# The third mixer channel of pairs 5 to 7 with plain weights, its taps on ScalarE and its sums on GpSimd

## The chip, the cores and the metric

One core of a Trainium2 chip runs the whole program. The metric is the device time of one execution in microseconds (us); before the change it is 496.37 us as the median of 3 runs (495.74 to 497.36). All work is in fp32 or in pairs of rounded fp32 parts.

## The reference, cut to what matters

One decoder layer over 16 sequences of 128 tokens with 128 features. The first block is the mixer: a projection to three channels of 128 features, a causal convolution of 3 taps over each channel, a product, a causal convolution of 4 taps, a gate and an output projection. Its sum with x is normalised and goes to a self attention and a cross attention (16 heads of 64 each), a feed-forward part and a last block of experts.

```python
x = einsum('bld,de->ble', u, W_in) + b_in
uc = dw_causal_conv(swapaxes(x, 1, 2), short_w, short_b)   # 3 taps, zeros before the start
q, k, v = uc[:, :D], uc[:, D:2*D], uc[:, 2*D:]
v = dw_causal_conv(k * v, inner_w, inner_b)                # 4 taps
y = einsum('bld,de->ble', swapaxes(q * v, 1, 2), W_out) + b_out
```

## The kernel before, in words

The mixer works on pairs of sequences (m = 0 to 7, 256 columns). The attentions work on items, one for each sequence of each attention: p = 0 to 31, 0 to 15 are self attention. Each engine has its own program, written out by hand in order, and a loop over turns p. The order of the calls is the order of execution on that engine; semaphores tie the engines together. The first five mixer pairs are started early, and the rest of the mixer is spread over the turns 0 to 10.

In turn p TensorE (PE in the profile) makes queries, keys and values of later items (`unit`, `v_half`), the transposes of item p-1's probabilities (`transposes`, line 570), the scores of item p+1 (`scores`, line 587), and P times V of item p-1 (`p_v`, line 602). VectorE (DVE) takes the score maxima of item p+1 (`maxima`, line 1172), ScalarE (ACT) its exponentials (`exps`, line 871, four heads a call), DVE the reciprocals of the sums (line 1182), and GpSimd (POOL) multiplies the probabilities by them (`normalise`, line 1574, four calls of 128x512 an item). `transposes` of item p in turn p+1 begin only when all maxima of item p+2 are made (line 568), since both use banks 2 and 3.

Of the mixer: channels 0 and 1 of pair m are projected in turn 2m-8, channel 2 in turn 2m-7 (`projection`). So pairs 5, 6 and 7 have their channels 0 and 1 in turns 2, 4, 6 and channel 2 in turns 3, 5, 7. Channels 0 and 2 use bank 4, channel 1 bank 5; `p_v` writes both banks, so it waits for the evictions (line 597). There are two ways to the 3 taps:

- With weights that hold the taps (w3): nine matmuls of 256 columns, three shifted inputs times three products of high and low parts (lines 652 to 654), one eviction by ACT with a bias (line 944), and a repair of the first two columns on POOL (`edges`, line 1620).
- With plain weights: three matmuls (lines 72 to 74), three evictions by ACT with the tap as scale (`projected`, lines 939 and 941), and two sums on POOL (`add_taps`, line 1644). `TAPPED` = 5: pairs 5 to 7 do so, but only their channels 0 and 1.

On POOL `keys_values(m)` stands at the end of turn 2m-7, behind the four `normalise` of that turn: sums of channel 1, repair of channel 2, the product KV (line 1636), sums of channel 0. Behind it come `output_bias`, `affine` and `next_residual` of the next turn, and that turn's `normalise`. On DVE `inner_convolution(m)` (lines 1269 and 1273, four instructions of 128x256) stands in turn 2m-6, behind the last `pt_out`, and ahead of that turn's last reciprocals and of the next item's maxima. `x_low` (line 1246) stands on DVE in odd turns ahead of `residual` and the last reciprocals; it needs `x_high` (line 926), which stands on ACT behind the eviction of channel 2 and `exps(p, 3)`.

## Time and profile before

| | |
|---|---|
| median of 3 runs | 496.37 us (495.74 to 497.36) |
| profiled execution, whole time | 495.88 us |
| its span, first to last instruction | 493.8 us |
| PE busy | 469.6 us (95%) |
| DVE busy | 380.1 us (77%) |
| ACT busy | 374.0 us (76%) |
| POOL busy | 271.1 us (55%) |
| granted TensorE clock, mean | 0.987 |
| shares of the chain that ended last | PE 68%, DVE 14%, ACT 9%, issue 5%, POOL 1% |

Busy time counts each engine by itself. The chain follows the end of the program back through whatever released each step, so a share in it is time that the end waited on. A timeline row gives start, duration, engine, line, operation and operands; in brackets stands how long the engine was idle before it and who ended that. The start of an instruction can lie a little before the end of the one ahead on the same engine.

### The profile page before, as it was taken

How to read it: one execution, taken by the hardware profiler on the slowest of the kernel's cores; microseconds unless marked ns; L12 is line 12 of the kernel's file. 1: busy time of each engine (PE TensorE's matmuls, PEld its weight loads, DVE VectorE, ACT ScalarE, POOL GpSimd, SP SyncE). 2: the span in 40 equal slices, each digit the busy share in tenths (PEclk: the TensorE clock that was granted, in tenths of full speed). 3: DMA queues.
4: the chain of work that ended last, by engine and by line, in shares of the span. 5: the costliest groups of instructions: out<-in, count | busy, mean ns of one | idle time of the engine just before them, and what ended most of it. 6: DMA issues, size and time to landing. Idle time of an engine off the chain costs nothing.

```text
span 493.8 us, 14159 instructions
## 1 busy us (share of the span) xinstructions
PE 469.6 (95%) x4632; PEld 431.1 (87%) x4632; DVE 380.1 (77%) x1828; ACT 374.0 (76%) x1407; POOL 271.1 (55%) x396
## 2 busy tenths in 40 slices
PE   7778999999999999999999999999999999999993
PEld 7778888989899999999999999999999998798872
DVE  3678778888888877887787777777777777647884
ACT  4547898888877788877778887777777776754866
POOL 5556357876768554555545455444444455534553
PEclk9899999999999999999999999999999999999996
DMA  8750000000000004000000000000000000600003
GB/s 233 239 206 1 1 3 1 2 2 2 1 3 2 2 2 126 2 3 1 3 1 2 2 2 3 1 2 2 2 2 2 1 4 1 171 24 0 9 12 101
DMA packets 15688, 14.58 MB, mean 30 GB/s; under 512 B 2816, under 2 KB 13056, under 8 KB 15488
## 3 DMA queue, kind: packets, MB, share of 16 engines
q1 hardware_dynamic: 14008, 13.19, 8.9%
q8 instruction: 38, 0.62, 0.6%
q10 hardware_dynamic: 1608, 0.49, 0.4%
q14 instruction: 34, 0.28, 0.2%
HBM read 12.23 MB, written 1.44 MB: 28 GB/s over the span
## 4 chain that ended last, share of the span: by engine, by line
PE 68%; DVE 14%; ACT 9%; issue 5%; POOL 1%; DMA 1%; ACTq 0%; SPq 0%; DVEq 0%; POOLq 0%
PE late_bank L570 9%; PE late_bank L618 9%; PE late_bank L587 9%; PE late_bank L602 8%; PE late_bank L72 8%; PE late_bank L73 7%; PE late_bank L74 7%; ACT P L871 5%; DVE P L1172 4%; PE late_bank L305 3%; DVE G L1273 1%; PE late_bank L627 1%; DVE at_PT L1198 1%; PE late_bank L652 1%; DVE at_k L1190 1%
## 5 line engine op out<-in xcount | busy, mean ns | idle before, releaser
L871 ACT ACTIVATE P<-P,at_negmax 128x128 f32<-128x128 f32 x512 | 199.0, 397 | 75.0 <-DVE at_negmax L1172 75.0
L1574 POOL TENSOR_TENSOR P<-P,at_inv 128x512 f32<-128x512 f32 x128 | 136.7, 1079 | 114.4 <-DVE at_inv L1182 114.3
L1198 DVE COPY at_PT<-late_bank 128x512 f32<-128x512 f32 x128 | 87.7, 688 | 35.6 <-PE late_bank L570 35.4
L1172 DVE CUSTOM_DVE_ANT_0 P<-late_bank,maskb 128x128 f32<-128x128 f32 x512 | 110.4, 286 | 2.5 <-PE late_bank L587 2.5
L871 ACT ACTIVATION_READ_ACCUMULATOR P<-P,at_negmax 128x1 f32 x512 | 100.3, 196 | 0.0
L570 PE MATMUL late_bank<-ident,P 128*128 128x128 f32 x512 | 76.3, 273 | 2.5 <-DVE at_negmax L1172 1.8
L570 PEld LDWEIGHTS late_bank<-ident,P 128*128 128x128 f32 x512 | 59.7, 140 | 9.1 <-issue 4.5
L587 PE MATMUL late_bank<-at_k,at_q 64*128 64x128 f32 x1024 | 65.8, 279 | 0.9 <-DVE at_k L1190 0.9
L602 PE MATMUL late_bank<-at_PT,V 128*64 128x128 f32 x1024 | 63.0, 276 | 2.0 <-ACT C L941 2.0
L587 PEld LDWEIGHTS late_bank<-at_k,at_q 64*128 64x128 f32 x1024 | 59.7, 188 | 4.8 <-issue 1.2
L602 PEld LDWEIGHTS late_bank<-at_PT,V 128*64 128x64 f32 x1024 | 55.3, 137 | 5.9 <-issue 2.4
L1190 DVE COPY at_k<-late_bank 128x512 f32<-128x512 f32 x64 | 44.1, 690 | 5.7 <-PE late_bank L74 4.8
L1172 DVE DVE_READ_ACCUMULATOR2_ANT at_negmax<- 128x1 f32 x512 | 42.7, 83 | 0.0
L1592 POOL TENSOR_TENSOR at_N<-at_N,row_ln_g 128x128 f32<-128x128 f32 x32 | 14.7, 460 | 48.4 <-DVE at_N L1223 48.4
L881 ACT ACTIVATE at_q<-late_bank 128x512 f32<-128x512 f32 x64 | 37.5, 586 | 2.3 <-PE late_bank L74 2.3
L890 ACT ACTIVATE V<-late_bank 128x512 f32<-128x512 f32 x64 | 37.5, 585 | 0.0
L898 ACT ACTIVATE at_OT<-late_bank 128x512 f32<-128x512 f32 x64 | 34.2, 586 | 2.9 <-PE late_bank L602 2.9
L618 PE MATMUL late_bank<-wo_sa,at_OT 128*128 128x128 f32 x256 | 31.4, 276 | 0.6 <-DVE x1T_lo L1309 0.6
L618 PE MATMUL late_bank<-wo_ca,at_OT 128*128 128x128 f32 x256 | 31.2, 275 | 0.0
L618 PEld LDWEIGHTS late_bank<-wo_sa,at_OT 128*128 128x128 f32 x256 | 29.9, 192 | 1.2 <-issue 1.2
L618 PEld LDWEIGHTS late_bank<-wo_ca,at_OT 128*128 128x128 f32 x256 | 29.9, 192 | 0.1
L1182 DVE RECIPROCAL at_inv<-at_total 128x4 f32<-128x4 f32 x128 | 21.6, 171 | 10.1 <-ACT P L871 9.9
(213 smaller groups left out, 1068.6 us busy)
## 6 DMA issues: line engine op xcount, KB each, us to landing
ctxT_raw<-in_ctxT SPq DMA_DIRECT2D x1, 1024.0 KB, 8.6
out<-xres SPq DMA_DIRECT2D x4, 224.0 KB, 2.5
x<-in_xT SPq DMA_DIRECT2D x1, 768.0 KB, 11.1
xres<-in_x SPq DMA_DIRECT2D x1, 768.0 KB, 14.7
tap_rows<-in_short_wT SPq DMA_DIRECT2D x3, 192.0 KB, 4.6
sa_wq_raw<-in_sa_wq SPq DMA_DIRECT2D x1, 512.0 KB, 7.9
sa_wk_raw<-in_sa_wk SPq DMA_DIRECT2D x1, 512.0 KB, 9.7
sa_wv_raw<-in_sa_wv SPq DMA_DIRECT2D x1, 512.0 KB, 11.7
```

Of the source, the lines that this page charges most:

```text
L72: nc.tensor.matmul(out, w.hi[wsel], x.hi[xsel], start=first, stop=False)
L570: last = nc.tensor.transpose(banks[T_BANK[g % 2]][:, h * 128:(h + 1) * 128], P[:, n % 2, HQ * g + h, :], k.ident[:])
L587: last = nc.tensor.matmul(score_bank(h), q[rows, t % 2, h // 2, pair], kk[rows, t % 2, h // 2, pair], start=True, stop=True)
L602: last = nc.tensor.matmul(banks[O_BANK[h // 8]][part:part + 64, h // 2 % 4 * 128:(h // 2 % 4 + 1) * 128], V[:, n % 2, h * DH:(h + 1) * DH] ...
L618: last = nc.tensor.matmul(banks[W_BANK][:, 0:128], OT[:, n % 2, c, :], out_w[att(n)][:, c, :], start=(c == 0), stop=(c == H // 2 - 1))
L871: last = nc.scalar.activation(P[:, n % 2, h, :], P[:, n % 2, h, :], ACT.Exp, scale=-1.0, bias=negmax[:, n % 2, h:h + 1], accum_out=total[: ...
L881: nc.scalar.activation(q[:, t % 2, u:u + 2, :], banks[UNIT_BANK[0]][:].rearrange("p (h l) -> p h l", h=2), ACT.Copy, scale=NEG_SCALE).then ...
L890: nc.scalar.activation(V[:, n % 2, half * 512:(half + 1) * 512], banks[V_BANK][:], ACT.Copy).then_inc(v_ok, 1)
L1172: last = nc.vector.tensor_tensor_reduce(P[:, n % 2, h, :], score_bank(h), k.maskb[:, cols(n)], scale=1.0, scalar=3.0e38, op0=ALU.add, op1= ...
L1190: nc.vector.tensor_copy(kk[:, t % 2, u - 1:u + 1, :], banks[UNIT_BANK[1]][:].rearrange("p (h l) -> p h l", h=2)).then_inc(k_ok, 1)
L1198: nc.vector.tensor_copy(PT[:, HQ * g:HQ * g + HQ, :], banks[T_BANK[g % 2]][:].rearrange("p (h l) -> p h l", h=HQ)).then_inc(pt_ok, 1)
L1574: nc.gpsimd.tensor_tensor(tile, tile, inv[:, n % 2, HQ * g:HQ * g + HQ].unsqueeze(2).to_broadcast([128, HQ, 128]), ALU.mult).then_inc(norm ...
```

## The change

Channel 2 of pairs 5 to 7 takes the plain way too: three matmuls instead of nine, three evictions on ACT instead of one, and two sums on POOL instead of the repair. `keys_values` now makes the sums of channel 1, then of channel 2, then KV. The tap tiles lose their two spare columns, so the shifted part is written at an offset and the rest stays zero; there are six of them instead of four, all cleared by POOL at the start, and the plain weights are split for 384 columns instead of 256. In the turns 2, 4 and 6 `exps(p, 3)` moves on ACT from between the evictions of channel 0 and channel 1 to behind both.

```diff
--- before.py
+++ after.py
@@ -162,6 +162,7 @@
 def allocate_projected(k, early):
 
     k.projected_tiles = k.sb(early, "C", [128, 2, 3, PAIR, L]), k.sb(early, "G", [128, PAIR, L])
+    k.late_tap = k.sb(early, "tapped21", [128, PAIR, L])
 
 
 def allocate_context_high(k, ctx):
@@ -231,8 +232,8 @@
     bias = k.sb(mixer, "conv_bias", [128, 3])
     edge = k.sb(mixer, "edge", [128, 3, 2])
     tap_b = k.sb(mixer, "tap_b", [128, 3, 3])
-    k.plain_w = k.split(mixer, "plain_w", [128, 2 * D])
-    k.tapped = tuple(tuple(k.sb(mixer, f"tapped{c}{j}", [128, PAIR, L + 2]) for j in range(2)) for c in range(2))
+    k.plain_w = k.split(mixer, "plain_w", [128, 3 * D])
+    k.tapped = [k.sb(mixer, f"tapped{i}", [128, PAIR, L]) for i in range(5)]
     inner = k.sb(mixer, "inner", [128, 4])
     inner_b = k.sb(mixer, "inner_b", [128, 1])
     KV = k.sb(mixer, "KV", [128, PAIR, L + 3])
@@ -366,7 +367,7 @@
             ctx, "ff", "gained_ok x4_ok z_normal_ok z_half_ok out_ok last_ok last_half_ok blank")
         moved, ze_last, shift_e_ok, minus_e_ok = k.sems(ctx, "ff", "moved ze_last shift_e_ok minus_e_ok")
         plain_hi, plain_lo, tapped_ok, blank_taps = k.sems(ctx, "mx", "plain_hi plain_lo tapped_ok blank_taps")
-        plain_w, tapped = k.plain_w, k.tapped
+        plain_w, tapped = k.plain_w, (k.tapped[0:2], k.tapped[2:4], (k.tapped[4], k.late_tap))
         block = ctx.enter_context(nc.Block())
 
         LN3, OUTER, INNER_NORM, OUT = 0, 1, 2, 3
@@ -641,7 +642,7 @@
                     wait(pe, c_ok, (3 * m, 3 * m, 3 * m + 1)[c])
                 if c == 1:
                     wait(pe, r1_ok, m - 1)
-                if c < 2 and m >= TAPPED:
+                if m >= TAPPED:
                     pe.wait_ge(plain_lo, 1)
                     now = np.s_[:, m % 2, :, 2:2 + L]
                     mm_split(nc, two(c_bank(m, c)), plain_w, np.s_[:, c * D:(c + 1) * D], xT, now).then_inc(c_mm, 1)
@@ -932,11 +933,11 @@
                 wait(act, y_ok, m - 1)
                 if m == 0 and c == FIRST_ORDER[0]:
                     act.wait_ge(bias_ok, 1)
-                if c < 2 and m >= TAPPED:
-                    act.wait_ge(blank_taps, 4)
-                    wait(act, tapped_ok, 4 * (m - TAPPED) - 2 * c)
+                if m >= TAPPED:
+                    act.wait_ge(blank_taps, 6)
+                    wait(act, tapped_ok, 6 * (m - TAPPED) - (0, 4, 2)[c])
                     for j in range(2):
-                        nc.scalar.activation(tapped[c][j][:, :, 2 - j:2 - j + L], two(c_bank(m, c)), ACT.Identity,
+                        nc.scalar.activation(tapped[c][j][:, :, 2 - j:], two(c_bank(m, c))[:, :, 0:L - 2 + j], ACT.Identity,
                                              bias=tap_b[:, c, j:j + 1], scale=taps[:, c, j:j + 1])
                     nc.scalar.activation(C[:, m % 2, c], two(c_bank(m, c)), ACT.Identity, bias=short_b[:, c:c + 1],
                                          scale=taps[:, c, 2:3]).then_inc(c_ok, 1)
@@ -1096,11 +1097,9 @@
                 if p == 0:
                     exps(p, 3)
                 projected(pair_of(p, PROJECT), 0)
-                if p % 2 == 0 and p:
-                    exps(p, 3)
                 projected(pair_of(p, PROJECT), 1)
                 projected(pair_of(p, PROJECT - 1), 2)
-                if p % 2:
+                if p:
                     exps(p, 3)
                 if p % 2 and p < NPAIR:
                     x_high((p + PROJECT + 1) // 2)
@@ -1629,9 +1628,9 @@
                     edges(m, np.s_[1:3])
                 else:
                     add_taps(m, 1)
-                    edges(m, np.s_[2:3])
-                    pool.wait_ge(tapped_ok, 4 * (m - TAPPED) + 2)
-                pool.wait_ge(fix_ok, m + 1 + min(m, TAPPED))
+                    add_taps(m, 2)
+                    pool.wait_ge(tapped_ok, 6 * (m - TAPPED) + 4)
+                pool.wait_ge(fix_ok, min(2 * m + 1, 2 * TAPPED))
                 wait(pool, g_ok, m)
                 nc.gpsimd.tensor_tensor(KV[:, :, 3:], C[:, m % 2, 1], C[:, m % 2, 2], ALU.mult).then_inc(kv_ok, 1)
                 if m >= TAPPED:
@@ -1640,16 +1639,16 @@
             def add_taps(m, c):
 
                 for j in range(2):
-                    wait(pool, tapped_ok, 4 * (m - TAPPED) + 2 * (1 - c) + j)
-                    nc.gpsimd.tensor_tensor(C[:, m % 2, c], C[:, m % 2, c], tapped[c][j][:, :, 0:L],
+                    wait(pool, tapped_ok, 6 * (m - TAPPED) + (4, 0, 2)[c] + j)
+                    nc.gpsimd.tensor_tensor(C[:, m % 2, c], C[:, m % 2, c], tapped[c][j][:],
                                             ALU.add).then_inc(tapped_ok, 1)
 
             def plain_weights():
 
                 pool.wait_ge(ld_win, 16)
-                nc.gpsimd.tensor_copy(plain_w.hi[:], w_in[:, 0:2 * D]).then_inc(plain_hi, 1)
+                nc.gpsimd.tensor_copy(plain_w.hi[:], w_in[:]).then_inc(plain_hi, 1)
                 pool.wait_ge(plain_hi, 1)
-                nc.gpsimd.tensor_tensor(plain_w.lo[:], w_in[:, 0:2 * D], f32(plain_w.hi[:]),
+                nc.gpsimd.tensor_tensor(plain_w.lo[:], w_in[:], f32(plain_w.hi[:]),
                                         ALU.subtract).then_inc(plain_lo, 1)
 
             def gate(m):
@@ -1660,7 +1659,7 @@
                     edges(m, np.s_[0:1])
                     pool.wait_ge(fix_ok, 2 * (m + 1))
                 else:
-                    pool.wait_ge(tapped_ok, 4 * (m - TAPPED + 1))
+                    pool.wait_ge(tapped_ok, 6 * (m - TAPPED + 1))
                 pool.wait_ge(g_ok, m + 1)
                 wait(pool, o1_mm, m)
                 nc.gpsimd.tensor_tensor(yT[:], C[:, m % 2, 0], G[:], ALU.mult).then_inc(y_ok, 1)
```

On ScalarE, turns 2 and 3, before (tapped00 to tapped11 are tap tiles of channels 0 and 1, late_bank4 and late_bank5 the mixer's banks, at_q and at_OT tiles of the attention; P is the probabilities):

```order
L939 ACTIVATE tapped01<-late_bank4,tap_b,taps 128x2x128
L941 ACTIVATE C<-late_bank4,short_b,taps 128x256
L871 ACTIVATE P,at_total<-P,at_negmax 128x128 x4
L939 ACTIVATE tapped10<-late_bank5,tap_b,taps 128x2x128
L939 ACTIVATE tapped11<-late_bank5,tap_b,taps 128x2x128
L941 ACTIVATE C<-late_bank5,short_b,taps 128x256
L871 ACTIVATE P,at_total<-P,at_negmax 128x128 x8
...
L944 ACTIVATE C<-late_bank4,conv_bias 128x256
L871 ACTIVATE P,at_total<-P,at_negmax 128x128 x4
L926 ACTIVATE xT_hi<-x1 128x2x128
```

The same stretch of ScalarE in the changed kernel, whose line numbers are one higher here (tapped4 and tapped21 belong to channel 2):

```order
L940 ACTIVATE tapped1<-late_bank4,tap_b,taps 128x2x127
L942 ACTIVATE C<-late_bank4,short_b,taps 128x256
L940 ACTIVATE tapped2<-late_bank5,tap_b,taps 128x2x126
L940 ACTIVATE tapped3<-late_bank5,tap_b,taps 128x2x127
L942 ACTIVATE C<-late_bank5,short_b,taps 128x256
L872 ACTIVATE P,at_total<-P,at_negmax 128x128 x12
...
L940 ACTIVATE tapped4<-late_bank4,tap_b,taps 128x2x126
L940 ACTIVATE tapped21<-late_bank4,tap_b,taps 128x2x127
L942 ACTIVATE C<-late_bank4,short_b,taps 128x256
L872 ACTIVATE P,at_total<-P,at_negmax 128x128 x4
L927 ACTIVATE xT_hi<-x1 128x2x128
```

The last four exponentials of turn 2 now stand with the eight of turn 3 behind the evictions, and two more evictions stand ahead of turn 3's last exponentials and of `x_high`.

On GpSimd, the end of turn 3 and the start of turn 4, before (C is the projected channels, P the probabilities):

```order
L1581 TENSOR_TENSOR at_rstd<-at_mv,half_neg 128x1
L1644 TENSOR_TENSOR C<-C,tapped10 128x256
L1644 TENSOR_TENSOR C<-C,tapped11 128x256
L1620 TENSOR_TENSOR C<-C,edge 128x2x2
L1636 TENSOR_TENSOR KV<-C 128x2x128
L1644 TENSOR_TENSOR C<-C,tapped00 128x256
L1644 TENSOR_TENSOR C<-C,tapped01 128x256
L1673 TENSOR_TENSOR xres<-xres,b_out 128x256
L1592 TENSOR_TENSOR at_N<-at_N,row_ln1_g 128x128
L1595 TENSOR_TENSOR at_X<-at_N,row_ln1_b 128x128
L1601 TENSOR_TENSOR xres<-at_X,row_ca_bo 128x128
L1574 TENSOR_TENSOR P<-P,at_inv 128x512 x4
```

And in the changed kernel, same place:

```order
L1643 TENSOR_TENSOR C<-C,tapped2 128x256
L1643 TENSOR_TENSOR C<-C,tapped3 128x256
L1643 TENSOR_TENSOR C<-C,tapped4 128x256
L1643 TENSOR_TENSOR C<-C,tapped21 128x256
L1635 TENSOR_TENSOR KV<-C 128x2x128
L1643 TENSOR_TENSOR C<-C,tapped0 128x256
L1643 TENSOR_TENSOR C<-C,tapped1 128x256
L1672 TENSOR_TENSOR xres<-xres,b_out 128x256
L1591 TENSOR_TENSOR at_N<-at_N,row_ln1_g 128x128
L1594 TENSOR_TENSOR at_X<-at_N,row_ln1_b 128x128
L1600 TENSOR_TENSOR xres<-at_X,row_ca_bo 128x128
L1573 TENSOR_TENSOR P<-P,at_inv 128x512 x4
```

Two sums of 128x256 have taken the place of the small repair, and everything behind them on this queue, the next turn's four multiplies of P included, stands behind them.

## Rows read from the trace of the kernel before

**Rows 1.** Waits of PE, 60 to 150 us: who waited for whom, total, times, longest

```profile
PE late_bank L602 <- ACT C L941: 2.0, 3, 0.8
PE late_bank L570 <- DVE at_negmax L1172: 1.0, 4, 0.3
```

**Rows 2.** Timeline of PE: projection of channel 2 in turn 3; first transposes of turns 5 and 9

```profile
83.38 0.29 PE L652 MATMUL late_bank<-xT_hi,w_hi 128*128 128x256 f32 x1
...
84.11 0.28 PE L72 MATMUL late_bank<-x1T_hi,sa_wk_hi 128*128 128x256 f32 x1
...
107.03 0.41 PE L570 MATMUL late_bank<-ident,P 128*128 128x128 f32 x2 [0.25 <-DVE at_negmax L1172]
...
161.00 0.41 PE L570 MATMUL late_bank<-ident,P 128*128 128x128 f32 x2
```

**Rows 3.** Timeline of ACT, turns 2 and 3

```profile
71.15 1.02 ACT L939 ACTIVATE tapped<-late_bank,tap_b,taps 128x256 f32<-128x256 f32 x2
...
72.50 0.42 ACT L871 ACTIVATE P<-P,at_negmax 128x128 f32<-128x128 f32 x1
...
84.41 0.47 ACT L944 ACTIVATE C<-late_bank,conv_bias 128x256 f32<-128x256 f32 x1
84.76 0.41 ACT L871 ACTIVATE P<-P,at_negmax 128x128 f32<-128x128 f32 x1
...
86.30 0.42 ACT L926 ACTIVATE xT_hi<-x 128x256 fp32r<-128x256 f32 x1
```

**Rows 4.** Timeline of DVE: last reciprocals of turn 2, x_low of turn 3

```profile
75.88 0.17 DVE L1182 RECIPROCAL at_inv<-at_total 128x4 f32<-128x4 f32 x1
...
87.64 0.40 DVE L1246 TENSOR_TENSOR xT_lo<-x,xT_hi 128x256 fp32r<-128x256 f32 x1
```

**Rows 5.** Timeline of POOL, end of turn 3 and start of turn 4

```profile
91.33 1.45 POOL L1644 TENSOR_TENSOR C<-C,tapped 128x256 f32<-128x256 f32 x2
92.74 0.21 POOL L1620 TENSOR_TENSOR C<-C,edge 128x4 f32<-128x4 f32 x1
93.08 0.73 POOL L1636 TENSOR_TENSOR KV<-C 128x256 f32<-128x256 f32 x1
...
97.38 2.04 POOL L1574 TENSOR_TENSOR P<-P,at_inv 128x512 f32<-128x512 f32 x2
```

**Rows 6.** Timeline of DVE, convolution of turn 4

```profile
99.34 0.40 DVE L1269 TENSOR_SCALAR G<-KV,inner,inner_b 128x256 f32<-128x256 f32 x1
99.78 1.53 DVE L1273 SCALAR_TENSOR_TENSOR G<-KV,inner,G 128x256 f32<-128x256 f32 x3
```

**Rows 7.** Timeline of DVE, convolution of an earlier pair, 42 us

```profile
41.92 0.48 DVE L1246 TENSOR_TENSOR xT_lo<-x,xT_hi 128x256 fp32r<-128x256 f32 x1
42.33 1.12 DVE L1269 TENSOR_SCALAR G<-KV,inner,inner_b 128x256 f32<-128x256 f32 x1
43.49 1.14 DVE L1273 SCALAR_TENSOR_TENSOR G<-KV,inner,G 128x256 f32<-128x256 f32 x1
```

**Rows 8.** Timeline of POOL at the same time

```profile
42.08 2.27 POOL L1574 TENSOR_TENSOR P<-P,at_inv 128x512 f32<-128x512 f32 x2
```

**Rows 9.** Timeline of POOL, turn 8

```profile
152.37 2.04 POOL L1574 TENSOR_TENSOR P<-P,at_inv 128x512 f32<-128x512 f32 x2
```

**Rows 10.** Timeline of DVE, convolution of turn 8

```profile
154.45 0.40 DVE L1269 TENSOR_SCALAR G<-KV,inner,inner_b 128x256 f32<-128x256 f32 x1
```

**Rows 11.** Timeline of POOL, start of the program

```profile
1.75 1.08 POOL L1762 MEMSET tapped<- 128x260 f32 x4
...
4.26 0.72 POOL L1652 TENSOR_TENSOR plain_w_lo<-w_in,plain_w_hi 128x256 fp32r<-128x256 f32 x1
```

**Rows 12.** Timeline of DVE, its first instruction

```profile
5.64 0.56 DVE L1253 TENSOR_TENSOR w_raw<-w_in,tap_rows 128x384 f32<-128x384 f32 x1 [5.64 <-DMA tap_rows<-in_short_wT]
```

**Rows 13.** Timeline of PE: its longest idle time after the start

```profile
16.14 0.35 PE L669 MATMUL late_bank<-w_out,yT 128*128 128x128 f32 x1 [2.19 <-issue]
```

**Rows 14.** Windows: length, busy time of PE, PEld, DVE, ACT, POOL, granted clock, DMA share, GB/s

```profile
17.26:20.68 3.42, 3.06 (x15) 2.77 (x14) 2.63 (x11) 2.19 (x4) 1.45 (x3) 0.50 0.49 136
```

## The prediction

> **What bounds the kernel now.** The page's busy times come first: TensorE is busy 95% of the span, so most turns are bound by it, but the change lies in the turns 2 to 8, and these have to be read by themselves. The waits of TensorE from 60 to 150 us [rows 1] show that it stands still there in two ways: three times before P times V, for the eviction of channel 1 (2.0 us in all), and four times before the first transposes of a turn, for VectorE's maxima (1.0 us in all). The second kind is the telling one. A turn after an even one starts when VectorE is done, as at 107.03 in turn 5 [rows 2]; whatever TensorE gains before that point is only waited away there. In the even turns 2, 4 and 6 the end is therefore set by VectorE, and behind it by ScalarE. In the odd turns 3, 5 and 7 nothing on TensorE waits after that point, and VectorE in its turn waits for TensorE's last keys and transposes. Turn 9 starts its transposes at 161.00 [rows 2] with no wait shown, but hardly any room either: its maxima come from the VectorE queue of turn 8, which is full.
>
> **TensorE, turns 3, 5, 7.** Nine matmuls become three. The last six took from 83.38 to 84.11 [rows 2], 0.73 us; three turns, 2.2 us at most.
>
> **ScalarE, turns 3, 5, 7.** The eviction of channel 2 took one slot of 84.76 - 84.41 = 0.35 us; the three plain ones take 72.50 - 71.15 = 1.35 us [rows 3]. So `exps(p, 3)` and `x_high` come 1.0 us later. ScalarE's queue is full from turn 3's first exponentials on, so these evictions can't start earlier though the bank is full sooner. `x_high` then starts at 87.30 and ends 0.42 us later, 87.72. VectorE's `x_low` started at 87.64 [rows 4], and without the change of ScalarE it would come 0.73 us earlier, since VectorE follows TensorE here. Now it waits for 87.72 plus a few hundredths: 0.12 us later than before. So TensorE's saving in turns 3 and 5 is lost in this wait. It can be worse: the reciprocals directly ahead of `x_low` do come 0.73 us earlier, so GpSimd starts the multiply that they release at about 87.1, and at 1.02 us for one (half of 2.04, [rows 5]) it still runs until about 88.1, when `x_low` wants to start. Whether a VectorE instruction waits for a running GpSimd one is shown at 42 us [rows 7, 8] and priced below. I take 0.4 us of loss for turn 3 and for turn 5 (bounds 0.1 and 0.5); in turn 7 there is no `x_low`, the last exponentials (1.0 us later) still come ahead of their reciprocals, and I take the full gain of 0.73 us (bound: nothing).
>
> The Trainium skill, page "SBUF — State Buffer", section "Who interferes with whom", says that a VectorE instruction with two SBUF inputs contends with a GpSimd instruction that reads SBUF, and that the loser is blocked for the whole instruction. No row here shows it alone for a plain TENSOR_TENSOR of VectorE that comes second: x_low at 41.92 took 0.48 instead of 0.40 us [rows 7, 4], which points the same way. By the rule turns 3 and 5 lose about 0.4 us each; by the bare wait for `x_high` 0.1 us each.
>
> **The moved exponentials, turns 2, 4, 6.** `exps(2, 3)` started at 72.50 [rows 3] and moves behind 1.35 us of evictions, so its last sum is ready near 75.5. The reciprocals that need it start at 75.88 [rows 4]. About 0.3 us of room is left, so the move costs nothing; if the room were gone, each 0.1 us would go straight to the maxima behind them. Its gain is that channel 1 is evicted 1.5 us earlier and P times V no longer waits. I price that gain at nothing: TensorE just reaches the wait for the maxima 0.6 to 0.8 us sooner, and waits there longer.
>
> **GpSimd, end of the odd turns.** The two sums of channel 1 took 91.33 to 92.74, 1.41 us; each of the second pair has to wait for the sum before it, so I take 1.5 us. The repair, 93.08 - 92.74 = 0.34 us less the wait that any KV has, about 0.2 us, goes [rows 5]. Everything behind is 1.3 us later. GpSimd had no idle time up to the two multiplies at 97.38, which ended at 99.42 [rows 5]. They now run from 98.7 to 100.7 (bounds of the shift: 1.1 and 1.5 us). GpSimd itself has room before its third multiply, so on its own queue this costs nothing. But VectorE's convolution starts at 99.34 [rows 6], that is exactly when these multiplies used to end.
>
> What then happens is shown at 42 us. There two such multiplies ran from 42.08 for 2.27 us [rows 8], and the convolution came in between: its first instruction took 1.12 instead of 0.40 us and the second 1.14 instead of 0.49 to 0.51 [rows 7, 6]. Each was held until the running multiply was over. The cost was 0.72 + 0.65 = 1.37 us. In turn 4 the first instruction comes some 0.6 us after the start of the first multiply instead of 0.25, so it is held about 0.35 to 0.5 us, and the second by the second multiply, 0.65 us. I take 1.1 us for each even turn. Below: 0.7 us, if the shift is small and only the second is held; above: 1.37 us.
>
> This sits on VectorE between `pt_out` and the reciprocals and maxima that release turn 5, where TensorE already waits. So the price is paid in full in turns 4 and 6. In turn 8 the same meeting occurs for pair 7: multiplies at 152.37 for 2.04 us [rows 9], convolution at 154.45 [rows 10], again one right behind the other before. Turn 9 has next to no room [rows 2], so I take 1.1 us there as well.
>
> **Start of the program.** Four clearings took 1.03 us [rows 11], 0.26 each; two more add 0.5. The subtraction of 0.72 us and the cast ahead of it grow from 256 to 384 columns, some 0.4 us together by an estimate from the subtraction. It ended at 4.98 and would end near 5.9. VectorE's first instruction starts at 5.64 [rows 12] and has everything behind it; held by the subtraction it loses 0.2 us (bounds: nothing, 0.35).
>
> **The sum.** 0.2 (start) + 2 x 0.4 (turns 3, 5) + 3 x 1.1 (turns 4, 6, 8) - 0.7 (turn 7) = +3.6 us. With the lower bounds 0 + 0.2 + 2.1 - 0.7 = +1.6; with the upper ones 0.35 + 1.0 + 4.1 = +5.5. On the profiled execution's 495.88 us that is 499.5. The median of the runs is 0.49 us above that execution, so the forecast is 500.0 us, with 498.0 to 501.9 as its own range.
>
> **Rivals.**
>
> *Nothing to measure.* The late multiplies don't hold the convolution, or VectorE has room that I don't see; then the terms left are 0.2 + 0.2 - 0.7, about 496.1 us. For it: all added work lies on engines at 55% and 76% busy, and the even turns' gain is waited away in any case. Against it: rows 7 and 8 show the same two instructions held by the same multiplies.
>
> *Faster.* TensorE is the bound in all these turns: the eighteen matmuls (2.2 us) go, and part of the 2.0 us of waits for the eviction [rows 1] too. All of it would be 4.2 us, 492.2; with the matmuls alone 494.2, which I take. For it: 95% busy. Against it: the waits for the maxima [rows 1] stand behind both savings, and `x_high` behind the new evictions. It decides only if VectorE's path gets no longer than before.
>
> *Slower still, by the clock.* TensorE's waits before turns 5 and 7 grow from 0.25 + 0.6 to about 2.0 us in one piece. After its idle 2.19 us at 16.14 [rows 13] the granted clock was 0.50, that is 1.2 instead of 2.4 GHz, from 17.26 for 3.4 us [rows 14]. Each such stretch would cost up to 1.7 us; with one or two of them about 502.5 us. Against it: the idle time here stands between full stretches.
>
> **How the numbers follow.** About 0.3% (1.5 us) is what a measurement of this kernel tells from no change. Chances: the collision forecast 0.64, the clock 0.07, nothing to measure 0.19, faster 0.10. Slower by over 0.3% gets the first two and hardly anything of the third, 0.70; within 0.3% 0.21, faster 0.09. The range reaches down to the time of the rival without a change, 496.2, and up to 501.9, which leaves out the faster rival, half of the one without a change, and most of the clock's.
>
> **What would show it.** In the changed profile line 1268 and the first of line 1272 (the convolution) should take about 0.8 and 1.1 us in turns 4, 6 and 8, with the multiplies of line 1573 beside them; elsewhere they stay at 0.40 and 0.49. TensorE's waits for the eviction should be gone, and those for the maxima should have grown to about 2 us before turns 5 and 7 and about 1 us before turn 9. `x_low` should show a wait for `x_high`, or over 0.7 us. TensorE's busy time falls by some 18 x 0.28 us of overlapping records without the span following. The forecast is wrong if the convolution keeps its durations, or if it grows and turn 5 still starts its transposes no later than before.

## The result and the profile after

The changed kernel takes 500.71 us as the median of 7 runs (499.2 to 503.91); the kernel before, beside it on the same chip, takes 496.37 us (495.74 to 497.84). The ratio is 1.009, with a 95% interval of 1.0067 to 1.0114: slower by 0.9%. The profiled execution took 500.64 us, its span is 498.6 us.

The head of the page, with busy time, share of the span and instructions of each engine:

```profile
span 498.6 us, 14136 instructions
...
PE 468.4 (94%) x4614; PEld 428.0 (86%) x4614; DVE 384.3 (77%) x1828; ACT 377.2 (76%) x1413; POOL 276.9 (56%) x401
```

Nothing here tells where 4.8 us of span come from. The waits of TensorE do, here from 60 to 165 us (who waited for whom: total, times, longest; from 60 to 150 us, as in [rows 1], the first two rows are the same):

```profile
PE late_bank L571 <- DVE at_negmax L1171: 3.3, 6, 0.7
PE late_bank L72 <- DVE at_negmax L1171: 2.6, 3, 1.2
PE late_bank L619 <- DVE x1T_lo L1308: 0.4, 2, 0.2
```

The wait for the eviction of channel 1, first of [rows 1], is gone. The waits for the maxima have grown from 1.0 us to 3.3 + 2.6 = 5.9 us. It now shows in two places, because `unit` (the projections of line 72) also waits for VectorE's maxima, which free its bank.

Now the convolution of turn 4, which answers to [rows 6], in the timeline of DVE (start, duration, line, operation, tiles, shape, count):

```profile
99.73 0.87 DVE L1268 TENSOR_SCALAR G<-KV,inner,inner_b 128x256 f32<-128x256 f32 x1
100.64 2.19 DVE L1272 SCALAR_TENSOR_TENSOR G<-KV,inner,G 128x256 f32<-128x256 f32 x3
102.74 0.17 DVE L1181 RECIPROCAL at_inv<-at_total 128x4 f32<-128x4 f32 x1
```

The same time on POOL, answering to [rows 5]:

```profile
91.73 3.23 POOL L1643 TENSOR_TENSOR C<-C,tapped 128x256 f32<-128x256 f32 x4
95.04 0.73 POOL L1635 TENSOR_TENSOR KV<-C 128x256 f32<-128x256 f32 x1
...
99.41 2.09 POOL L1573 TENSOR_TENSOR P<-P,at_inv 128x512 f32<-128x512 f32 x2
```

The two multiplies ran from 97.38 to 99.42 and now run from 99.41 to 101.50. The convolution, which came right behind them at 99.34, now stands at 99.73, that is inside them. Its first instruction takes 0.87 us and not 0.40, its three others 2.19 us together and not 1.53 (1.14, 0.49 and 0.48). Turn 8 shows the same (0.76 and 1.14 us):

```profile
158.09 0.76 DVE L1268 TENSOR_SCALAR G<-KV,inner,inner_b 128x256 f32<-128x256 f32 x1
158.88 1.14 DVE L1272 SCALAR_TENSOR_TENSOR G<-KV,inner,G 128x256 f32<-128x256 f32 x1
```

And `x_low` of turn 3, answering to the second of [rows 4]:

```profile
87.79 0.65 DVE L1245 TENSOR_TENSOR xT_lo<-x,xT_hi 128x256 fp32r<-128x256 f32 x1 [0.75 <-ACT xT_hi L927]
```

It waits 0.75 us for `x_high` and then takes 0.65 us instead of 0.40.

To see which turn costs what, I take the same instruction in both traces and subtract its start before from its start after (the offset). TensorE's first transposes of turn 5 and of turn 9 answer to [rows 2]:

```profile
108.54 0.41 PE L571 MATMUL late_bank<-ident,P 128*128 128x128 f32 x2 [0.74 <-DVE at_negmax L1171]
...
165.65 0.52 PE L571 MATMUL late_bank<-ident,P 128*128 128x128 f32 x3 [0.74 <-DVE at_negmax L1171]
```

The offset is 108.54 - 107.03 = 1.51 us at turn 5 and 165.65 - 161.00 = 4.65 us at turn 9. From turn 9 to 440 us it stays at 4.6 to 4.7 us. By turns, read in the same way (to some 0.02 us) at VectorE's instructions that begin and end a turn, such as `at_k` and `at_R`: start 0.04, turn 3 +0.36, turn 4 +1.12, turn 5 +0.35, turn 6 +1.12, turn 7 +0.67, turn 8 +1.0.

Turn 7 stands out, since it should have gained 0.73 us. Three windows around it (length, TensorE's busy time and instructions, granted clock, DMA share, GB/s):

```profile
134.73:138.11 3.38, 1.43 (x12) 1.00 0.00 0
138.11:141.53 3.42, 3.42 (x16) 0.50 0.01 2
141.53:144.95 3.42, 3.42 (x31) 1.00 0.00 0
```

In the middle one the granted clock is 0.50, that is 1.2 instead of 2.4 GHz, and 16 matmuls are done instead of 31. It costs 0.67 + 0.73 = 1.4 us: the turn loses 0.67 us where its repeats at full clock, below, gain 0.73. Ahead of it TensorE had stood still for 1.21 and for 0.74 us:

```profile
135.94 0.36 PE L72 MATMUL late_bank<-x1T_hi,sa_wq_hi 128*128 128x256 f32 x1 [1.21 <-DVE at_negmax L1171]
...
137.63 0.65 PE L571 MATMUL late_bank<-ident,P 128*128 128x128 f32 x4 [0.74 <-DVE at_negmax L1171]
```

### The profile page after: what moved, and what is told of

The parts are those of the page before. It is cut to its first block, busy times and chain, and to the rows that moved or that the text cites. A ratio compares the mean times of both kernels' runs of the same rounds, so it can differ in the third digit from the quotient of the medians.

```text
span 498.6 us, 14136 instructions
## 1 busy us (share of the span) xinstructions
PE 468.4 (94%) x4614; PEld 428.0 (86%) x4614; DVE 384.3 (77%) x1828; ACT 377.2 (76%) x1413; POOL 276.9 (56%) x401
## 4 chain that ended last, share of the span: by engine, by line
PE 63%; DVE 14%; ACT 13%; issue 6%; POOL 2%; DMA 1%; ACTq 0%; SPq 0%; DVEq 0%; POOLq 0%
PE late_bank L619 9%; PE late_bank L571 9%; PE late_bank L588 8%; PE late_bank L603 8%; PE late_bank L72 7%; ACT P L872 7%; PE late_bank L74 7%; PE late_bank L73 7%; DVE P L1171 3%; PE late_bank L306 3%; DVE G L1272 2%; ACT at_OT L899 1%; DVE at_k L1189 1%; PE late_bank L628 1%; DVE at_PT L1197 1%
```

## The experiments

The theory: nearly the whole loss is the meeting of GpSimd's late multiplies with VectorE's convolution in turns 4, 6 and 8, with a smaller one at `x_low`. The rivals: the moved exponentials do it, or the evictions on ScalarE, or the clock.

**The order alone.** The kernel before with only the exponentials moved:

```diff
-                if p % 2 == 0 and p:
-                    exps(p, 3)
                 projected(pair_of(p, PROJECT), 1)
                 projected(pair_of(p, PROJECT - 1), 2)
-                if p % 2:
+                if p:
                     exps(p, 3)
```

> The kernel before, with only the last four exponentials of turns 2, 4 and 6 moved behind both evictions. Theory (GpSimd's later multiplies hold VectorE's convolution): the move is free and brings nothing; TensorE's waits for the eviction (2.0 us) go and its waits for the maxima grow from 1.0 to about 3.0 us, time within 0.5 us of the kernel before, the convolution stays at 0.40 and 0.49 us. Rival (the longer ScalarE queue ahead of the exponentials is what costs): the reciprocals wait for ScalarE, and the time rises by 1 us or more.

Measured: 496.68 us beside 496.65, ratio 1.0002 (0.9984 to 1.002). TensorE's waits from 60 to 165 us:

```profile
PE late_bank L570 <- DVE at_negmax L1170: 2.4, 4, 0.7
...
PE late_bank L72 <- DVE at_negmax L1170: 0.2, 1, 0.2
```

The wait for the eviction (2.0 us) is gone, the waits for the maxima are larger by 1.6 us (2.6 instead of 1.0), and the offset stays at 0.97 us from turn 2 to turn 9. The move is worth nothing in either direction. (The 0.97 us come from before turn 2, where the clock's stretches at 0.50 lie elsewhere in this execution.)

**The exponentials put back.** The changed kernel with these lines reversed:

> The changed kernel with the exponentials of turns 2, 4 and 6 put back between the two evictions. Theory (the meeting on GpSimd and VectorE costs): time unchanged within 0.7 us of the changed kernel, that is 499.5 to 501.2; the convolution in turns 4, 6, 8 still takes about 0.87 and 1.14 us; TensorE waits for the eviction again, about 2 us in three, and less for the maxima. Rival (the moved exponentials cost): back by 2 us or more, to 498.5 or less.

Measured: 501.09 us beside 496.65, ratio 1.0097 (1.0069 to 1.0124). The wait for the eviction is back:

```profile
PE late_bank L603 <- ACT C L942: 2.2, 3, 0.7
```

By turns the offset grows by 0.37, 1.13, 0.37, 1.14, -0.73 and 1.0 us from turn 3 to turn 8: the changed kernel's terms, with turn 7 at its full gain since this profile has no stretch at half clock there. The moved exponentials have no part in the loss.

**Without the sums of channel 0.** The changed kernel with the first two taps of channel 0 left out, so that two sums fewer stand on GpSimd ahead of the next turn's multiplies:

```diff
-                if m >= TAPPED:
-                    add_taps(m, 0)
```

The semaphore counts, left out here, go with it.

> The changed kernel without GpSimd's two sums of channel 0 for pairs 5 to 7 (their first two taps are left out of channel 0). GpSimd then has as many sums ahead of the next multiplies as the kernel before. Theory: the multiplies come at most 0.2 us later than before, the convolution is back at 0.40 and 0.49 us, and the 3.3 us of turns 4, 6 and 8 go: 497.3 us, or 496.0 if the clock stays at 1.00. Turns 3 and 5 still lose about 0.35 us each in x_low. Rival (the loss is ScalarE's or TensorE's): above 499 us.

Measured: 497.32 us beside 496.65, ratio 1.0007 (0.9986 to 1.0027). The convolution of turn 4:

```profile
99.75 0.41 DVE L1268 TENSOR_SCALAR G<-KV,inner,inner_b 128x256 f32<-128x256 f32 x1
100.19 1.53 DVE L1272 SCALAR_TENSOR_TENSOR G<-KV,inner,G 128x256 f32<-128x256 f32 x3
```

It has its old durations, at nearly the same place (99.75 and 99.73). TensorE, VectorE and ScalarE have the work of the changed kernel; only GpSimd's is 1.5 us shorter in each of these turns. Turns 4, 6 and 8 cost nothing, turns 3 and 5 still 0.36 and 0.35, turn 7 gains 0.73. This is the experiment that shows the cause.

**Two additions behind the multiplies.** GpSimd's `next_residual` and `output_bias` (0.46 and 0.74 us) moved behind the second multiply in turns 4, 6 and 8, all work kept:

```diff
-                next_residual(p - 3)
+                late = p in (4, 6, 8)
+                if not late:
+                    next_residual(p - 3)
                 for g in range(QUARTERS):
+                    if g == 2 and late:
+                        next_residual(p - 3)
+                        output_bias(pair_of(p, PROJECT - 2))
                     normalise(p, g)
...
-                output_bias(pair_of(p, PROJECT - 1))
+                if p not in (3, 5, 7):
+                    output_bias(pair_of(p, PROJECT - 1))
```

> The changed kernel, with GpSimd's output_bias (0.74 us) and next_residual (0.46 us) of turns 3 to 8 moved behind the first two multiplies of the turns 4, 6 and 8. Theory: the two multiplies come 1.2 us earlier, 0.4 us later than in the kernel before instead of 1.6; the convolution's first instruction takes about 0.7 us, its second 0.49; each even turn costs 0.3 to 0.4 instead of 1.1 us, so the time falls by 2.2 us, and by up to 1.4 us more if the clock stays at 1.00 in turn 7: 497.0 to 498.5. Rival (TensorE's stretch at the low clock and the longer ScalarE queue are the whole loss, the meeting is hidden): no more than 0.5 us, unless the clock changes.

Measured: 499.82 us, ratio 1.0056 (1.0039 to 1.0073). I had expected 497.0 to 498.5, so this was too hopeful. VectorE and GpSimd in turn 4:

```profile
101.41 0.66 DVE L1268 TENSOR_SCALAR G<-KV,inner,inner_b 128x256 f32<-128x256 f32 x1
102.10 1.95 DVE L1272 SCALAR_TENSOR_TENSOR G<-KV,inner,G 128x256 f32<-128x256 f32 x3
```

```profile
99.88 2.04 POOL L1573 TENSOR_TENSOR P<-P,at_inv 128x512 f32<-128x512 f32 x2
101.88 0.50 POOL L1600 TENSOR_TENSOR xres<-at_X,row_ca_bo 128x128 f32<-128x128 f32 x1
102.34 0.91 POOL L1672 TENSOR_TENSOR xres<-xres,b_out 128x256 f32<-128x256 f32 x1
```

The first instruction still meets the end of the second multiply, and the next two (0.56 and 0.83 us, the last 0.48) meet the two additions that I had moved. These turns cost 0.66, 0.66 and 0.55 us instead of 1.12, 1.12 and 1.0. So GpSimd's additions hold the convolution too, not the multiplies alone, and such work has to be moved out of the convolution's way, not only behind something.

**`x_high` and `x_low` ahead.** `x_high` ahead of the three evictions of channel 2, and `x_low` ahead of the mixer's statistics, so that it comes before the reciprocals that release a multiply:

```diff
                 projected(pair_of(p, PROJECT), 1)
+                if p % 2 and p < NPAIR:
+                    x_high((p + PROJECT + 1) // 2)
                 projected(pair_of(p, PROJECT - 1), 2)
                 if p:
                     exps(p, 3)
-                if p % 2 and p < NPAIR:
-                    x_high((p + PROJECT + 1) // 2)
...
-                mixer_statistics(pair_of(p, OUTPUT))
-                reciprocals(p, 2)
                 if p % 2:
                     x_low((p + PROJECT + 1) // 2)
+                mixer_statistics(pair_of(p, OUTPUT))
+                reciprocals(p, 2)
```

> The changed kernel with x_high ahead of channel 2's evictions on ScalarE and x_low ahead of the mixer's statistics on VectorE, in the odd turns. Theory: in turns 3 and 5 VectorE no longer waits for x_high nor for a running multiply, so they win 0.7 us each as turn 7 does instead of losing 0.36; turn 4, 6 and 8 lose 1.1 us each as before: about 2.2 us less than the changed kernel, 498.5, the meeting with 0.87 and 1.14 us still there. Rival (the odd turns' loss is in the exponentials that stand 1.0 us later on ScalarE): no gain, since x_high ahead of them makes them another 0.35 us later; 500.7 or more.

Measured: 498.35 us beside 496.33, ratio 1.0036 (1.0017 to 1.0055), as expected.

```profile
87.35 0.41 DVE L1245 TENSOR_TENSOR xT_lo<-x,xT_hi 128x256 fp32r<-128x256 f32 x1
```

No wait, no hold. Turn 3 gives 0.88 us and turn 5 0.86 us where the changed kernel lost 0.36 and 0.35; turns 4, 6 and 8 cost 1.14, 1.12 and 1.01 as in the changed kernel.

**Tap tiles of 130 columns.** The change had also made the tap tiles 128 columns wide; here they have 130 again, with the same values:

```diff
-    k.tapped = [k.sb(mixer, f"tapped{i}", [128, PAIR, L]) for i in range(5)]
+    k.tapped = [k.sb(mixer, f"tapped{i}", [128, PAIR, L + 2]) for i in range(5)]
```

The sixth tile and the accesses to all of them, left out here, change likewise.

> The changed kernel with tap tiles of 130 columns a sequence instead of 128, as in the kernel before; what is written and read is the same. In the kernel before a sum took 0.69 us, in the changed one 0.73 to 0.80. If the tile's layout is the reason, the sums are back at 0.69 and the multiplies come 0.3 us earlier (shift 1.3 instead of 1.6 us), the convolution's first instruction is held longer, about 0.3 us more, since it meets the first multiply nearer to its middle; the time stays within 0.7 us of the changed kernel in either case. If the sums keep 0.73 us, the layout is not it.

Measured: 498.52 us, ratio 1.0046 (1.0025 to 1.0068), which is some 2 us less than the changed kernel (500.71; 500.4 in its repeat below), where I had expected at most 0.7. The groups of line 1643 from 84 to 165 us, count, busy time, mean ns and idle time before, first the changed kernel, then this one:

```profile
L1643 POOL TENSOR_TENSOR C<-C,tapped 128x256 f32<-128x256 f32 x18 | 13.4, 744 | 0.9
```

```profile
L1643 POOL TENSOR_TENSOR C<-C,tapped 128x256 f32<-128x256 f32 x18 | 12.5, 696 | 0.9
```

A sum takes 696 ns from the wider tiles and 744 from the plain ones (the kernel before, which had the wider ones, 688). Six of them make 0.3 us, and by that much the multiplies come earlier. In turn 4:

```profile
99.76 0.58 DVE L1268 TENSOR_SCALAR G<-KV,inner,inner_b 128x256 f32<-128x256 f32 x1
```

```profile
99.15 2.09 POOL L1573 TENSOR_TENSOR P<-P,at_inv 128x512 f32<-128x512 f32 x2
```

The convolution's first instruction takes 0.58 us instead of 0.87. I had expected the contrary, a longer hold: it starts 0.61 us behind the multiply and not 0.32, so less of that multiply is left to wait for. Turns 4, 6 and 8 cost 0.84, 0.83 and 0.71 us, together 0.86 less. So 0.86 of the 3.24 us that the change costs in these turns come from its narrower tap tiles and not from the added sums. For the rest of the 2 us the clock is the likely reason, not shown: 6 of this kernel's 10 executions had a mean clock of 0.993 or more, of the changed kernel's 19 only one, and of 84 of the kernel before 21.

**All of it together.** The wider tiles, `x_high` and `x_low` ahead, `next_residual` at the end of turns 4, 6 and 8, and `output_bias` of turns 3, 5 and 7 two turns later, behind the second multiply of turns 5, 7 and 9, where VectorE has no convolution. These moves on GpSimd are new:

```diff
-                next_residual(p - 3)
+                if p not in (4, 6, 8):
+                    next_residual(p - 3)
                 for g in range(QUARTERS):
+                    if g == 2 and p in (5, 7, 9):
+                        output_bias(pair_of(p, PROJECT - 3))
                     normalise(p, g)
...
+                if p not in (3, 5, 7):
+                    output_bias(pair_of(p, PROJECT - 1))
+                if p in (4, 6, 8):
+                    next_residual(p - 3)
```

> The changed kernel with x_high and x_low ahead as in x_ahead, tap tiles of 130 columns, GpSimd's next_residual of turns 4, 6, 8 at the end of its turn and output_bias of turns 3, 5, 7 two turns later behind its second multiply, so that neither stands between the sums and the multiplies nor beside the convolution. Theory: the multiplies come about 0.1 us later than in the kernel before, the convolution takes 0.40 to 0.5 and 0.49 us, the even turns lose 0.1 us each and the odd ones win 0.7 us each: 1.9 us faster than the kernel before, 494.5. Rival (extra ScalarE work in the odd turns costs by itself): no faster than the kernel before.

Measured: 493.88 us (492.68 to 495.68) beside 496.33, ratio 0.9956 (0.9935 to 0.9976). This beats both kernels. The convolution of turn 4, the multiplies beside it, and TensorE's waits:

```profile
98.63 0.40 DVE L1268 TENSOR_SCALAR G<-KV,inner,inner_b 128x256 f32<-128x256 f32 x1
99.07 1.53 DVE L1272 SCALAR_TENSOR_TENSOR G<-KV,inner,G 128x256 f32<-128x256 f32 x3
```

```profile
96.80 2.04 POOL L1573 TENSOR_TENSOR P<-P,at_inv 128x512 f32<-128x512 f32 x2
```

```profile
PE late_bank L571 <- DVE at_negmax L1171: 2.2, 3, 0.7
...
PE late_bank L72 <- DVE at_negmax L1171: 0.2, 1, 0.2
```

The multiplies end at 98.84, and the convolution that begins at 98.63 has all its old durations. At turn 9 the offset is -2.3 us: the matmuls' gain in turns 3, 5 and 7 (three times 0.73, and 0.1 to 0.15 more in turns 3 and 5) arrives at last.

**One more step.** The same with the cross attention's `weight_low` (1.2 us on VectorE) moved from turns 2, 4 and 6 to turns 9, 10 and 11:

> As best2, and the three low parts of the cross attention's weights (line 1314, 1.2 us each on VectorE) made in turns 9 to 11 instead of 2, 4, 6. The even turns are bound by VectorE and ScalarE, and the late exponentials leave 0.3 us of room ahead of their reciprocals, so each even turn wins about 0.3 us and not 1.1: another 1.0 us, 493.5. If turns 9 to 11 have no room for them on VectorE, the gain is lost there and TensorE waits for maxima in these turns.

Measured: 494.06 us, ratio 0.996 (0.9939 to 0.998), no better than the one before. Its offset is -2.67 us at turn 9, but by turn 10 it is -1.73 and stays: 0.94 us is given back where the work now stands. So each even turn did gain, but turns 9 and 10 have no room for the work. TensorE waits 0.65 us for VectorE's `x1T_lo` there, and 0.20 us in the variant before:

```profile
177.00 2.02 PE L619 MATMUL late_bank<-wo_sa,at_OT 128*128 128x128 f32 x16 [0.65 <-DVE x1T_lo L1308]
```

```profile
176.42 2.02 PE L619 MATMUL late_bank<-wo_sa,at_OT 128*128 128x128 f32 x16 [0.20 <-DVE x1T_lo L1308]
```

**The changed kernel again.** Three more profiles of it, the first with ten executions for the median, to look at the stretch at half clock:

> The changed kernel once more, without an edit. Its first profiled execution had 1.4 us of its loss from a stretch at half clock at 138 us, behind TensorE's waits of 1.21 and 0.74 us before turn 7. Theory A: that stretch is chance, as such stretches come in every kernel here; then it is not there again (or stands elsewhere), the offset against the kernel before falls by 0.7 us in turn 7 and is about +3.2 us at turn 9, and the executions with a clock of 0.99 or more are about as frequent as for the kernel before (a third to a half), at 498 to 499 us. Theory B: the longer waits bring it about; then a stretch at half clock stands at 106 or 136 us again, the offset at turn 9 is 4.5 us or more, and executions with a high clock are rarer. Median 500.0 to 500.7 us by either.

> The changed kernel a third time, one profile. As for the run before it: by theory A no stretch at half clock between 60 and 170 us and an offset of +3.2 us at turn 9; by theory B one at 106 or 136 us and 4.5 us or more.

> The changed kernel a fourth time, one profile. Of three executions two had a stretch at half clock behind the wait of turn 7, at 138.1 and 140.0 us. By chance alone this one has none; if the wait brings it about, more often than not it has one, and its offset against the kernel before at turn 9 is 1.4 us larger than its offset at turn 7 would give.

Measured: 500.4 us beside 496.97 (ratio 1.0075, 1.0046 to 1.0103), and single times of 502.21 and 503.43. The windows from the long wait on, in the second, third and fourth profile of the changed kernel:

```profile
135.84:139.20 3.36, 1.40 (x12) 1.00 0.00 0
139.20:142.60 3.40, 3.40 (x27) 1.00 0.01 2
```

```profile
136.39:139.99 3.60, 1.64 (x13) 1.00 0.01 2
139.99:143.41 3.42, 3.42 (x16) 0.50 0.00 0
```

```profile
106.76:110.33 3.57, 1.61 (x12) 1.00 0.00 0
110.33:113.75 3.42, 3.42 (x15) 0.50 0.00 0
```

The second has none; the third has it in turn 7 again, the fourth in turn 5. Where it stands it costs 1.4 us again. Without it the second profile's offset grows by 3.2 us from turn 2 to turn 9.

**A longer wait.** The changed kernel with the convolution's first instruction issued three times in turns 4, 6 and 8:

```diff
+                extra = 2 if m >= 5 else 0
+                for j in range(1 + extra):
+                    if j:
+                        vec.wait_ge(g_part, done + j)
                     nc.vector.tensor_scalar(G[:], KV[:, :, 3:3 + L], inner[:, 3:4], inner_b[:, 0:1],
                                             ALU.mult, ALU.add).then_inc(g_part, 1)
```

> The changed kernel with the first instruction of the convolution issued three times instead of once in turns 4, 6 and 8: some 0.9 us more on VectorE there, and so TensorE's waits before turns 5 and 7 grow from 1.2 to about 2.1 us. Both theories expect +2.7 us for the three turns themselves. Theory A (a stretch at half clock in turn 7 is chance): nothing more, median 503.1 to 503.6 us and no such stretch between 100 and 150 us. Theory B (the long wait brings it about): one behind the wait of turn 5, of turn 7 or of both, 1.4 us or more each, median 504.5 us or more, and the offset against the kernel before jumps by that much behind the wait.

Measured: 503.86 us (502.44 to 504.61) beside 496.16, ratio 1.0141 (1.0104 to 1.0177), between the two theories. The three turns cost 1.98, 1.97 and 1.84 us, some 0.85 more each than in the changed kernel. TensorE's waits are 1.48 and 1.49 us and not 2.1, since a part of VectorE's delay already meets TensorE earlier (0.56 us of waiting for `at_R` ahead of turn 5), and the stretch is there in turn 7:

```profile
136.18:138.07 1.89, 0.41 (x4) 1.00 0.00 0
138.07:141.48 3.41, 3.02 (x15) 0.50 0.01 2
```

Turn 7 costs 0.08 us instead of gaining 0.73, so the stretch costs some 0.8 us here, less than before: TensorE waits only 0.39 us for the next maxima, and inside the stretch. So four of the five profiles in which TensorE waits 1.2 us or more before turns 5 and 7 have such a stretch right behind one of these waits; of the nine others (the kernel before and eight variants, whose waits there are at most 1.0 us) none has one between 60 and 170 us. In the kept traces it goes with the long wait, but each of these five has two such waits and one stretch at most, and the longer waits of this last variant brought no second one. One run speaks against the wait as the whole story: with the exponentials put back no wait is longer than 0.75 us and the kept trace has no stretch there, yet the kernel is no faster (501.09 us), and 7 of its 10 executions have a mean clock of 0.985 or less, as 10 of the changed kernel's 19 and only 17 of 84 of the kernel before. Where their stretches lie isn't on record. So that the long wait brings the stretch about is suggested and not shown, and what makes it come in one execution and not in the next, the runs don't tell.

## Why the prediction was right

The direction, the mechanism and the size held: forecast 500.0 us, measured 500.71. That the size came out so near is in part luck, in the first point and in the sum. Point by point:

- *The convolution in turns 4, 6, 8: 1.1 us each.* Measured 1.12, 1.12 and 1.0; leaving out the sums of channel 0 takes them away. But two steps on the way were off and made up for each other. I had the multiplies of turn 4 from 98.7, a shift of 1.3 us (bounds 1.1 and 1.5); they started at 99.41, 2.03 us later. A sum took 744 ns in the mean and not the 0.7 us of [rows 5], which makes 0.3 us, and 0.4 us is what turn 3 had already lost and VectorE with it. So the convolution came 0.32 us behind the start of the multiply and not 0.6, and was held 0.47 us (0.87 - 0.40), inside my 0.35 to 0.5. At 0.6 us it would have been less: with the wider tiles it came 0.61 us behind, was held 0.18 us, and the turn cost 0.84 us. A hold is shorter than what is left of the GpSimd instruction, here by 0.25 us in both runs, and at 42 us too (0.97 us were left, the hold was 0.72). The second instruction was held 0.65 us as at 42 us [rows 7].
- *Turns 3 and 5: 0.4 us each.* Measured 0.36 and 0.35, by both parts of the argument: a wait for `x_high`, then 0.25 us of hold by the running multiply. With both made earlier, neither is there.
- *The moved exponentials: nothing.* Measured nothing, with the order alone and with the order put back. TensorE reached the next wait earlier and waited there longer, 2.6 instead of 1.0 us.
- *The start: 0.2 us.* The two profiles differ by only 0.04 us there, but that is chance and doesn't refute the term. The subtraction on GpSimd ended at 5.86, as forecast, and VectorE's first instruction is held by it; everything behind it follows, ScalarE's cast at once. Below is this instruction, first in the changed kernel, then in the kernel before with the order alone, whose start is that of the kernel before:

```profile
5.54 0.73 DVE L1252 TENSOR_TENSOR w_raw<-w_in,tap_rows 128x384 f32<-128x384 f32 x1 [5.54 <-DMA tap_rows<-in_short_wT]
```

```profile
5.35 0.56 DVE L1251 TENSOR_TENSOR w_raw<-w_in,tap_rows 128x384 f32<-128x384 f32 x1 [5.35 <-DMA tap_rows<-in_short_wT]
```

It starts when `tap_rows` has landed, and that varies from execution to execution: from 4.94 to 6.20 us in the 14 kept traces, 5.64 in that of the kernel before [rows 12]. In the changed kernel and its variants it ends at 6.27 to 6.30 in eleven of twelve traces whenever it started, and takes up to 1.34 us for it (in the twelfth it started at 6.20 and took 0.56). So the start costs 0.37 us against the trace with the order alone, 0.08 against that of the kernel before, and about 0.3 us at the median landing of 5.44; the forecast's 0.2 lies between.
- *Turn 7: a gain of 0.7 us.* By itself right: -0.72 to -0.74 in the eight profiles of the changed kernel and its variants whose clock stayed at 1.00 there, the one with `weight_low` moved apart. In the profiled execution it was a loss of 0.67, by the stretch at half clock. I had that as a rival with a chance of 0.07, and argued against it that the idle time stands between full stretches. Of four profiles of the changed kernel three have such a stretch once. The idle time came in two pieces, 1.21 and 0.74 us, and not in one. The price was about right (1.4 us; I had up to 1.7), the chance too small.
- *The sum.* 0.04 + 0.71 + 3.24 - 0.73 = 3.26 us without the stretch, where I had 3.6, and 4.66 with it. The medians differ by 4.34 us, or by 3.43 in the repeat. So the terms of the forecast were 0.3 us too large together, and half of that is the start, which by the paragraph above was no error. What the medians have above 3.26 us, 0.2 to 1.1 us, is left to the clock (mean 0.985 in the changed kernel's 19 executions, 0.989 in 84 of the kernel before), which the sum left out.
- *A sign that failed.* TensorE's busy time should have fallen by some 5 us (18 times 0.28); it fell by 1.2 us (469.6 to 468.4). The busy time counts overlapping matmuls once, so no more than the 0.73 us a turn of the sum could show, 2.2 in all, and stretches at half clock, which lengthen it, lie elsewhere in the two executions.

The rival without a change fell since VectorE has no room behind the convolution: TensorE waits for the maxima right behind it. The faster rival was half right, and the run with all of it together shows it: the 2.2 us of the eighteen matmuls are real, and come through once VectorE's path gets no longer.

Of the rule that the Trainium skill gives ("SBUF — State Buffer", section "Who interferes with whom"), by which the loser of such a meeting is blocked for the whole instruction, the trace agrees on VectorE's side: its instructions stretch to just behind the end of the running multiply (100.60 and 101.78 behind 100.45 and 101.50), while the two multiplies hardly lose, 2.09 us beside them and 2.04 alone. `x_low` at 0.65 us is the case that no row of before showed alone.

## What to carry to other kernels

When work is added to an engine that is half idle, don't ask whether it has room in the mean; ask what its queue will then be executing at the moment when the critical engine runs its SBUF-to-SBUF instructions. Here 1.6 us more on GpSimd, none of it waited for, cost VectorE 1.1 us in each of three turns. Moving two small additions out of the way, with an operand produced earlier and the tap tiles wide again, turned +0.9% into -0.4%. And a gain on an engine that waits right behind it is none until the wait is gone. A last point is on reading two profiles: their difference at one place can be a chance of the execution, as with the landing of `tap_rows` here, so look at the same place in the other runs before a term is called wrong.

## What was not expected of the hardware

- A GpSimd addition of 128 x 256 in fp32 took 744 ns in the mean with the second operand in tiles of 2 x 128 columns, and 696 ns with the same columns in tiles of 2 x 130 (18 of each). Whether it is the width of the tile or where the tiles then lie, the runs don't tell apart.
- A stretch of 3.4 us at a granted clock of 0.50 in an otherwise busy part of the program, behind waits of 1.21 and 0.74 us (1.49 us in one variant), in four of five profiles with such waits, at 1.4 us each (0.8 in that variant). The stretch of the kernel before at 17.26 us [rows 14] cost next to nothing: the trace with the order alone, which has none there, is 0.29 us ahead at 16.9 us and 0.32 at 28.0.
- VectorE is held by small GpSimd additions just as by the multiplies: with 0.50 and 0.91 us of additions beside it, the rest of the convolution took 1.95 us instead of 1.53.
- What is held ends a little behind what holds it, by less than its own duration: 0.15 us for the convolution's first instruction (0.40 alone), 0.28 for its second (0.48 alone) and for `x_low` (0.40 alone), 0.41 for VectorE's first instruction of the program (0.56 alone).
